# Splitting the spills around two small transfers, a ring turn written out, and expert weights moved behind the last small transfer

## What is computed

```python
def _L0_ffn_ref(x, ...):             # b, s, d = 2, 1024, 128; H = 16 heads of 8
    qkv = x @ w_qkv
    scores = einsum('bhqd,bhkd->bhqk', q, k) / sqrt(8)        # causal
    attn = softmax(where(causal, scores, finfo.min))
    o = einsum('bhqk,bhkd->bhqd', attn, v) ... @ w_o
    h = layernorm(x + o, g1, b1)
    probs = softmax(h @ wg)          # 8 experts, the top 2 are used
    h1 = gelu(einsum('bsd,edf->ebsf', h, w1) + bb1)           # F = 512
    y = einsum('ebsf,efd->ebsd', h1, w2) + bb2
    moe = einsum('ebsd,bse->bsd', y, w)
    return layernorm(h + moe, g2, b2)

x = x + 0.5 * _L0_ffn_ref(_layernorm(x), ...)
x = x + _L0_attn_ref(_layernorm(x), ...)     # attention over 96 selected keys
x = x + 0.5 * _L0_ffn_ref(_layernorm(x), ...)
return x
```

## Time and profile before

| | us |
|---|---|
| median of 3 runs | 1655.86 (1653.0 to 1657.17) |
| the profiled execution | 1672.07, span 1670.3 |
| TensorE busy in the span | 1422.6 (85%) |
| VectorE busy | 1239.8 (74%) |
| ScalarE busy | 981.1 (59%) |
| GpSimd busy | 463.3 (28%) |

### The profile page before, as it was taken

The page is one execution under the profiler, slowest core; times in us unless marked ns, Lnnn a source line. Parts: engine busy times, 40 slices in busy tenths (PEclk is TensorE's granted clock), DMA queues, the critical chain, the costliest instruction groups (busy, mean ns, idle before and its releaser), DMA issues.

```text
span 1670.3 us, 31774 instructions
## 1 busy us (share of the span) xinstructions
PE 1422.6 (85%) x10664; PEld 927.1 (56%) x10664; DVE 1239.8 (74%) x2576; ACT 981.1 (59%) x1792; POOL 463.3 (28%) x755
## 2 busy tenths in 40 slices
PE   5799998799994843899899999997799998799994
PEld 3445554577773311556565555665455554577773
DVE  5577885697778586677888787765678885588787
ACT  2366667478882573356565545553366665488883
POOL 4122232100002037345555544623122222100000
PEclk9699999799997865899999988997699998699997
DMA  4411110032202236012132212211511120022200
GB/s 110 142 36 46 47 48 4 1 106 73 75 26 79 51 96 150 23 55 65 38 83 66 63 38 61 75 36 26 145 38 47 47 66 10 1 103 76 76 26 25
DMA packets 64379, 99.26 MB, mean 59 GB/s; under 512 B 21027, under 2 KB 44259, under 8 KB 62198
## 3 DMA queue, kind: packets, MB, share of 16 engines
q1 hardware_dynamic: 54614, 79.97, 16.5%
q0 software_dynamic: 8192, 16.79, 4.0%
q10 hardware_dynamic: 1440, 0.80, 0.2%
HBM read 69.00 MB, written 10.69 MB: 48 GB/s over the span
## 4 chain that ended last, share of the span: by engine, by line
PE 55%; DVE 13%; ACT 10%; issue 6%; DMA 5%; SPq 5%; DVEq 4%; ACTq 1%; POOL 0%; POOLq 0%
PE twin L1039 9%; PE twin L1211 5%; PE twin L1029 5%; PE twin L891 5%; PE twin L869 5%; PE twin L836 4%; DMA ffn<-arena 4%; ACT arena L1278 3%; DVEq L1899 2%; ACT experts L1361 2%; PE twin L1239 2%; PE twin L1227 2%; PE twin L1192 2%; ACT arena L1359 2%; PE twin L1255 2%
## 5 line engine op out<-in xcount | busy, mean ns | idle before, releaser
L1278 ACT ACTIVATE arena<-twin 128x1024 f32<-128x1024 f32 x288 | 294.0, 1024 | 186.9 <-PE twin L869 185.2
L792 POOL DMA_INDIRECT arena<-kv_rows,IDX x256 | 250.7, 979 | 218.5 <-PE twin L1258 148.6
L1562 DVE TENSOR_REDUCE arena<-twin 128x8 f32<-128x1024 f32 (+1 forms) x160 | 195.4, 1225 | 84.8 <-PE twin L836 43.7
L1359 ACT ACTIVATE arena<-twin,bias 128x512 f32<-128x512 f32 x256 | 185.2, 723 | 60.7 <-PE twin L1029 60.6
L1611 DVE TENSOR_TENSOR experts<-arena,experts 128x512 fp32r<-128x512 f32 x256 | 170.1, 689 | 61.9 <-ACT experts L1361 60.3
L1029 PE MATMUL twin<-experts,experts 128*128 128x512 f32 x768 | 197.3, 403 | 5.9 <-ACT experts L1361 5.8
L752 POOL TENSOR_SCALAR_AFFINE_SELECT arena<-arena 128x256 f32<-128x256 f32 x256 | 99.6, 407 | 321.2 <-ACT arena L1278 321.2
L1361 ACT ACTIVATE experts<-twin,bias 128x512 fp32r<-128x512 f32 x256 | 186.5, 729 | 0.0
L1039 PE MATMUL twin<-experts,experts 128*128 128x512 f32 x768 | 183.2, 390 | 1.4 <-DVE experts L1611 1.4
L836 PE MATMUL twin<-ffn,ffn 64*128 64x128 f32 (+3 forms) x1152 | 160.4, 362 | 27.2 <-ACT arena L1278 13.7
L1552 DVE TENSOR_REDUCE arena<-twin 128x2 f32<-128x1024 f32 x128 | 153.1, 1223 | 31.3 <-PE twin L836 28.1
(11 more groups left out here) (261 smaller groups left out, 2211.5 us busy)
## 6 DMA issues: line engine op xcount, KB each, us to landing
arena<-wt_rows SPq DMA_DIRECT2D x16, 1024.0 KB, 4.9
arena<-in_L_ffn_w SPq DMA_DIRECT2D x32, 256.0 KB, 5.3
XT<-idx_rows SPq DMA_DIRECT2D x16, 512.0 KB, 5.1
ffn<-q_rows SPq DMA_DIRECT2D x48, 128.0 KB
ffn<-k_rows SPq DMA_DIRECT2D x48, 128.0 KB
ffn<-ffn SPq DMA_DIRECT2D x64, 64.0 KB
q_rows<-ffn SPq DMA_DIRECT2D x8, 512.0 KB, 6.4
k_rows<-ffn SPq DMA_DIRECT2D x4, 1024.0 KB, 8.5
```

The source lines that it names most:

```text
L792: pool.indirect_dma_start(G[d % GR][:, g, :], None, kv_rows, bass.IndirectOffsetOnAxis(ap=IDX[:, q, k * GB + g:k * GB + g + 1], axis=0))\
L1278: act.activation(PT[(UNITS * buf + u) % PT_RING].rearrange("p s n -> p (s n)"), twin[2 * u % S_RING][:, :], ACT.Exp, scale=float(HD) ** -0 ...
L1359: act.activation(H1[tb % 2][:, f, :], bank[f][:, :], ACT.Gelu_apprx_tanh, bias=bias1[buf][:, f:f + 1])
L1562: dve.tensor_reduce(to, scores.rearrange("p (s t k) -> p s t k", s=2, t=to.shape[2]), AX_X, ALU.max).then_inc(max_done, 1)
```

## The change

SP's program changes, and no other engine's. In both layers the spill of batch 0 moves ahead of the loads of pair 3, and the spill of batch 1 behind the maxima of pair 1. The loop's first turn (pairs 4 to 7) is written out with constants; its sp_rows waits for the spill of batch 0 alone. In layer 2 the four transfers with the weights of experts 0 and 1 move behind the maxima of pair 15.

```diff
         def sp_rows(sp, c, it, buf):
 
-            for b in range(B):
+            for b in range(1 if isinstance(it, int) else B):
                 sp.wait_ge(rows_spilled[b], (PARTS + 1) * 16 * (c + 1))
...
             sp_maxrows(sp, c, 0, 0)
+            sp_spill(sp, c, 0)
             sp_first(sp, c, 3, rows_loaded[3])
             sp_values(sp, 3, 3)
-            for b in range(B):
-                sp_spill(sp, c, b)
-            with sp.Fori(1, PAIRS // RING) as i:
+            for k in range(RING):
+                sp_maxrows(sp, c, k + 1, (k + 1) % RING)
+                if k == 0:
+                    sp_spill(sp, c, 1)
+                sp_rows(sp, c, RING + k, k)
+            with sp.Fori(2, PAIRS // RING) as i:
                 for k in range(RING):
                     sp_maxrows(sp, c, i * RING + k - (RING - 1), (k + 1) % RING)
                     sp_rows(sp, c, i * RING + k, k)
+            for it in range(PAIRS - RING + 1, PAIRS):
+                sp_maxrows(sp, c, it, it % RING)
             if c:
                 for e in range(2):
                     sp_expert(sp, c, e, e)
-            for it in range(PAIRS - RING + 1, PAIRS):
-                sp_maxrows(sp, c, it, it % RING)
```

## The result

The changed kernel took 1632.11 us (median of 4 runs, 1627.92 to 1640.68), against 1656.51 us of the kernel before (4 runs beside it): a ratio of 0.9852 with a 95% interval of 0.9808 to 0.9895, or 24.4 us less. The forecast was 1635.1 us, 20.8 us less. Two more measurements of the same kernel, on two other chips, gave 0.9899 (0.9860 to 0.9938) and 0.9881 (0.9844 to 0.9917): on a kernel that takes 1784 and 1781 us there these are 18 and 21 us.

What follows compares the result with a forecast made beforehand. TensorE was taken as the bound, waiting for small maxima transfers and then running at low clock. Gains of 22.05 us less 1.0 gave 21.05; 0.99 of it, 20.8, off 1655.86 gave 1635.1 us, range 1629 to 1647.

Steps and rivals of the forecast that it cites:

- Stall, pair 1: TensorE's stall ahead of pair 1 shrinks to 0.20 us, gaining 4.1 us in layer 1 and 3.7 in layer 2.
- Cover for spill 0 and pair 3's loads: SP's queue is clear at 64.8, before pair 1's maxima flow at 67.2; cover 2.4 us, nothing charged.
- Clock: TensorE keeps its upper clock level through pair 1, gaining 5.15 us in layer 1 and 3.63 in layer 2.
- Pair 2's near miss: Queue clear at 82.2 behind rows 4, pair 2's maxima could flow at 82.0; 0.5 us charged in each layer.
- part 2: SP's first ring turn written out with constants: cost 0, at worst a microsecond of fetching in each layer, covered.
- Weights: Layer 2's expert weights behind the last maxima: transpose gap 20.12 to 14.61 us, 5.5 gained; cover 11 us, cost 0.
- Sum: Gains over both layers put at 22.05 us, less 2 x 0.5, so 21.05; 0.99 of it taken, 20.8.
- Rival (a): The stall moves to pair 2, maxima 2 us late and the clock falls there; gain 9.3, 1646.7 us; chance 0.13.
- (b): Stalls go, but the clock still falls in these pairs; gain 9.8, 1646 us; chance 0.08.
- (c): Spill 0 and pair 3's loads still block pair 1's maxima; only the weights' 5.5 is left, 1650.4 us; chance 0.07.
- (d): Slower: spill 1 ahead of rows 4 stalls pair 2 from 9.1 us on, clock lost; 1662.5 us at 10; chance 0.03.

Runs made afterwards that it cites:

- the second try of the spills alone: The changed kernel, but with layer 2's expert weights back in their old place ahead of pair 13's maxima; measured 0.9935 against the kernel before.
- the filler kernel: The changed kernel plus seven matmuls, result unread, where TensorE waits for the layer norm behind attention; 0.9834 against the kernel before, median 1753.27 us.

## Why the prediction was right

**Stall, pair 1.** Predicted issue of the maxima at 65.6, start at 68.96 behind 0.20; measured 65.50, 68.80 and 0.23. Layer 2's stall 0.17. The 4.1 and 3.7 us were right to a tenth.

**Cover for spill 0 and pair 3's loads.** The prediction had the queue clear at 64.8, with first bytes of the maxima at 67.2. SP's issues of these loads took 10.07 us instead of 6.33, behind the spill, and the DMA share is 0.16 in 64 to 66: clear in time for the maxima, which show no delay. That SP's issues take longer behind a spill was not in the working; here it idles until 65.5, so it cost nothing.

**Clock.** Pair 1 lasts 14.60 us, as assumed. But the 5.15, 3.63 and 5.5 us come from one trace of before, one draw for each stall, and this was the weakest place of the sum. Over the five traces with the old order of spills the clock cost ahead of pair 1 has a mean of about 3.5 us in layer 1 and 4.5 in layer 2; the gap at pair 13 is 4.7 us over a clean one in the mean of the three that kept the weights' place as well. Of the nineteen stalls of 1.9 us and more sixteen had a clock cost of 3.4 to 5.1, and three of 0 to 0.9.

**Pair 2's near miss.** The sum had the queue clear at 82.2 and charged 0.5 us a layer. The tail of rows 4 shows as predicted, 0.13 of the engines and 51 GB/s in 80 to 82. What 82 to 84 moved, 13 GB/s or 26 KB, is about the maxima's own 24 KB, so the tail was out at about 82, just when their first bytes were due. TensorE started 3.19 us behind their issue, as it does with an empty queue, so in this trace nothing was due of the two half microseconds. Two traces with the same order of spills and rows had stalls of 0.44 and 0.85 us there, with TensorE 3.52 and 3.93 us behind the issue (the second try of the spills alone, and the filler kernel). So the charge lies within what occurs, and it was a near miss indeed. The Trainium skill, page "DMA: Bandwidth & Descriptors", section "Why a DMA increments its semaphore by 16 and not by 1", would have the tail and the maxima share the lowest-numbered engines. The two late cases agree with a wait for the tail; no run here has a tail long enough to show it.

**The turn.** For the microsecond of fetching that part 2 names as its worst case no row stands; alone the turn measured 1.0001.

**Weights.** The gap is 14.28 us, 5.8 less than in the first trace (5.5 predicted, with pair 2's 14.61 for a clean gap where the end of the layer has 14.3). Cover of the moved transfer: issued by 1376.4, wanted at 1389.0, nothing waited. But across cases a stall of 2 us has a clock cost in most and not all, so the part is worth 2.0 to 7.7 us by the gaps of the five traces with the weights in their old place, 4.2 by the mean of stretches, and in time it could not be told from 0 when alone.

**Sum.** The terms add up to 22.08 and not 22.05, which changes nothing. The forecast was 21.05 us on the stretches; the stretches gave 21.1, three measurements 24.4, 18.0 and 21.2. That the stretches agree to a tenth is luck: layer 1 was put at 8.75 us and gave 7.7, layer 2 at 12.3 and gave 13.4. The mechanism was right, stall and low clock behind it, and the sizes of single terms were off by up to 1.7 us in one direction or the other. Rival (a) was built as an experiment and gives back some half of the gain; (b) did not occur in any of the traces with the new order; (c) had its margin; for (d) the spill would have had to run at a third of the 371 GB/s that it shows.

## What to carry to other kernels

A small transfer that an engine waits for should be issued ahead of the bulk transfers in the same queue. Where the bulk can't be moved as a whole, split it; write down for each bulk transfer when the queue is clear again and when the next small one is ready. Cost a stall of TensorE as its length plus the low clock behind it, here 2 to 4 us plus mostly 3.4 to 5.1, and expect the second term to be nearly absent in some executions (3 of 19 stalls). And don't judge a change by the spans of two traces: here two traces differed by 44 us, of which the change made some 21.

## What the runs showed that I had not expected

- The same kernel took 1659 us on one chip and 1781 to 1784 us on two others, all of it in the selection stage: its stretch took 623 to 637 us in the faster traces and 752 to 766 in the slower, while attention of the outer parts was equal to a microsecond or so for the same kernel. In the slower traces the granted clock of the whole was 0.877 to 0.892, in the faster ones 0.903 to 0.930. The cause wasn't followed up.
- SP's issues of transfers get slower behind a spill: eight issues of 64 KB took 10.07 us behind 2 MB and 6.33 us without it.
- TensorE's clock also falls without a long stall right ahead. In the filler kernel it fell at 306.1, 1.6 us into the router's matmuls of 8 columns; ahead of them it had waited 0.87 us, and 0.36 to 0.37 before each of the last three groups of transposes. It stayed low for 6.8 us with TensorE busy all the time (0.59 in 308 to 314).
